# Both halves of a two-matmul accumulation wait for the later of their inputs

## The reference

```python
x = x + layernorm(attention(layernorm(x)))     # 16 heads of 8, 1024 keys
x = x + layernorm(ffn(layernorm(x)))

# ffn: three cycles, each of them on all 1024 tokens
gf = global_net(mean of x over the tokens)
for _ in range(3):
    h = gelu(out @ w1 + b1)      # 256 -> 256
    h = gelu(h @ w2 + b2)        # 256 -> 128, contracted over 256
    h = gelu(h @ w3 + b3)        # 128 -> 64
    tf = sigmoid(h @ w4 + b4)    # 64 -> 1
    coupling = 0.1 + adaptive_range * (0.7 * gf + 0.3 * tf - 0.5) * 2.0
    out = out + coupling * twist(out)
```

## Time and profile before

| | us |
|---|---|
| median of 3 runs | 3420.03 |
| the profiled execution, its own time | 3420.04 |
| its span (first to last instruction) | 3418.2 |
| TensorE busy | 3280.1 (96%) |
| VectorE busy | 2961.0 (87%) |
| ScalarE busy | 2896.0 (85%) |
| GpSimd busy | 976.6 (29%) |

### The profile page before, as it was taken

How to read it: one execution, slowest core, us unless ns; L and a number is a source line. 1 busy time by engine, 2 the same in 40 slices (tenths; PEclk the granted TensorE clock), 3 DMA queues, 4 the chain that set the end, 5 groups by cost and what they waited for, 6 DMA issues and landing times.

```text
span 3418.2 us, 55797 instructions
## 1 busy us (share of the span) xinstructions
PE 3280.1 (96%) x19328; PEld 931.1 (27%) x19328; DVE 2961.0 (87%) x5517; ACT 2896.0 (85%) x3806; POOL 976.6 (29%) x1382
## 2 busy tenths in 40 slices
PE   6989999999999999999999999999999999999987
PEld 2222232322323232232322323232232322323222
DVE  7999989888898988989888898988989888898942
ACT  3868979798897979889798897979989798896975
POOL 5012060421506033060421406033060421505024
PEclk7998999999999999999999999999999999999999
DMA  3111111121112111111121111111121121111001
GB/s 89 26 41 43 37 44 32 43 49 43 51 33 54 39 49 43 43 50 32 43 50 43 51 33 50 41 46 47 36 57 33 43 49 44 38 32 50 7 22 37
DMA packets 97337, 144.71 MB, mean 42 GB/s; under 512 B 49312, under 2 KB 59936, under 8 KB 89248
## 3 DMA queue, kind: packets, MB, share of 16 engines
q1 hardware_dynamic: 93360, 123.83, 13.7%
q0 software_dynamic: 3696, 17.31, 2.7%
HBM read 34.61 MB, written 32.51 MB: 20 GB/s over the span
## 4 chain that ended last, share of the span: by engine, by line
PE 69%; DVE 14%; ACT 8%; issue 4%; SPq 2%; POOL 2%; DMA 1%; DVEq 0%; POOLq 0%
PE heads_ps L503 24%; PE ring_ps L470 15%; PE scoresT_ps L488 11%; DVE max_parts L949 10%; PE scoresT_ps L590 7%; ACT p_sb L700 4%; PE scoresT_ps L595 3%; DVE stats L960 2%; PE scoresT_ps L598 2%; ACT headsT L709 1%; PE scoresT_ps L601 1%; PE ring_ps L532 1%; SPq L337 1%; PE scoresT_ps L518 1%; PE heads_ps L470 1%
## 5 line engine op out<-in xcount | busy, mean ns | idle before, releaser
L949 DVE TENSOR_REDUCE max_parts<-ring_ps 128x1 f32<-128x512 f32 x3741 | 2365.5, 682 | 230.0 <-PE ring_ps L470 171.1
L700 ACT ACTIVATE p_sb<-scoresT_ps 128x1024 f32<-128x1024 f32 x2048 | 1970.2, 1025 | 84.6 <-PE scoresT_ps L488 60.8
L470 PE MATMUL ring_ps<-k_rows,q_rows 48*128 48x512 bf16 x3741 | 1078.0, 385 | 23.5 <-DVE max_parts L949 14.4
L503 PE MATMUL heads_ps<-p_sb,v_sb 128*9 128x512 f32 x8192 | 1073.3, 596 | 17.9 <-ACT headsT L709 11.9
L488 PE MATMUL scoresT_ps<-q_rows,k_rows 51*128 51x512 bf16 x4096 | 1021.8, 384 | 15.0 <-ACT p_sb L700 7.5
L470 PEld LDWEIGHTS ring_ps<-k_rows,q_rows 48*128 48x128 bf16 x3741 | 263.5, 94 | 1319.9 <-DVE max_parts L949 1209.6
L1210 POOL CAST max_wide<-max_all 128x16 bf16<-128x16 f32 x128 | 25.1, 196 | 1753.7 <-DVE max_all L955 1753.7
L590 PE MATMUL scoresT_ps<-state,w 128*128 128x512 f32 x736 | 365.4, 619 | 5.9 <-DVE state L1013 3.9
L488 PEld LDWEIGHTS scoresT_ps<-q_rows,k_rows 51*128 51x128 bf16 x4096 | 207.7, 94 | 243.7 <-ACT p_sb L700 219.9
L811 ACT ACTIVATE p_sb<-scoresT_ps,b 128x512 f32<-128x512 f32 x180 | 123.5, 686 | 165.6 <-PE scoresT_ps L590 164.6
L503 PEld LDWEIGHTS heads_ps<-p_sb,v_sb 128*9 128x9 f32 x8192 | 124.7, 89 | 289.6 <-issue 278.6
(11 more groups left out here) (206 smaller groups left out, 2757.7 us busy)
## 6 DMA issues: line engine op xcount, KB each, us to landing
q_rows<-parts SPq DMA_DIRECT2D x744, 32.0 KB
k_rows<-parts SPq DMA_DIRECT2D x744, 32.0 KB
x_sb<-in_x SPq DMA_DIRECT2D x16, 1024.0 KB, 4.9
x_in<-in_x SPq DMA_DIRECT2D x15, 1024.0 KB, 5.1
out<-x_sb SPq DMA_DIRECT2D x15, 1024.0 KB, 3.9
out<-x_in POOLq DMA_DIRECT2D x15, 1024.0 KB, 7.8
q_rows<-max_rows SPq DMA_DIRECT2D x512, 3.0 KB
feat_h<-headsT SPq DMA_DIRECT2D x512, 16.0 KB
```

What stands on the lines that cost most here:

```text
L470: e.matmul(ring_bank(max_taken, u + 1), q_rows[rows, slot, pair, h * BANK + qb * P:h * BANK + (qb + 1) * P], k_rows[rows, slot, pair, kh * ...
L503: m = e.matmul(heads_ps[32 * j:32 * j + DH + 1, :], v_sb[:, b % 2, kb, 4 * (group % NG) + j, 0:DH + 1], p_sb[:, n % 2, j, :], start=(kb == ...
L700: e.activation(p_sb[:, n % 2, 2 * two:2 * two + 2, :].rearrange("p h n -> p (h n)"), scoresT_ps[:, 2 * two * BANK:(2 * two + 2) * BANK], A ...
L949: e.tensor_reduce(max_parts[:, gi % 2, kh, col:col + 1], bank_of(max_taken, u + 1), AX.X, ALU.max).then_inc(max_taken, 1)
```

## The change

In layer 2 the wait for the hidden features leaves the loop over f. One wait, for the later of the two gelus (m = 0 and m = 1), stands ahead of both matmuls. Operands, order of the matmuls, banks and the semaphore's increments stay as they are.

```diff
                 if layer == 2:
+                    e.wait_ge(hid_done[k], max(end_of(before, cycle, 1, c, m) for m in range(2)))
                     for f in range(2):
-                        e.wait_ge(hid_done[k], end_of(before, cycle, 1, c, f))
                         o = e.matmul(ps, w2[:, f, :], hidden[k][:, 0, 2 * c + f, :], start=(f == 0), stop=(f == 1))
```

## The result

The changed kernel takes 3441.31 us (median of 6 runs, 3439.81 to 3444.48) against 3420.03 (6 runs, 3418.41 to 3421.84): a ratio of 1.0063, 95% interval 1.0053 to 1.0074. The forecast was 3435.9 with a range of 3429 to 3441. The direction is right, and so is the mechanism in the stages; the size is too small, above all in the ending: the median lies 0.3 us above the range, and the loss is 21.3 us instead of 15.9.

What follows compares the result with a forecast made beforehand. TensorE was taken to bound the coupling stages (busy 67.64 of 69.10 us), with nothing behind winning delays back. 7.4 + 5.8 + 0.3 + 2.4 = 15.9 us on 3420.0 gave 3435.9 us, range 3429 to 3441.

Steps and rivals of the forecast that it cites:

- The pairs in the stages: Coupling stages, c = 0: 0.53 us per delayed pair; 7.4 us for cycle 2, 5.8 for cycle 0, 0.3 for cycle 1.
- The ending: Pairs of batches 14 and 15: 1.7 + 0.5 + 0.2 = 2.4 us, with bounds of 0 and 5.2.
- the clock: TensorE: its granted clock falling where it is 1.00 now was named as a sign that the prediction is wrong; no size.
- Half absorbed: Rival, cycle 0 of the stages: VectorE's reductions take up its delay; 5.8 us less, 3430.1 us; chance 0.10.
- not slower: Rival: the attention stage makes the stages' lateness good; 3420.0 to 3422.4 us; chance 0.05, of which 0.01 for faster.
- It costs more: Rival: nothing covered in stages 0, 8, 9, whole 0.86 in the ending, costlier restarts; up to 3443.1 us; chance 0.08.
- the pull-ahead: TensorE: first weight load done before the wait ends, 0.11 us less in 25 pairs, 3433.1 us; left out of the sum.

Runs made afterwards that it cites:

- e3: Kernel before with the joined wait only in cycle 0, c = 0, of the 14 coupling stages; 3428.59 us, one run.
- e8: Changed kernel with layer 2 no longer waiting separately for its bank; 3438.74 us, ratio 1.0055.
- e1: Kernel before with the joined wait only in the ending (batches 14 and 15); 3426.3 us, ratio 1.0012.
- e10: Changed kernel with two added matmuls ahead of each joined c = 0 wait of the ending; 3442.96 us, ratio 1.0062.
- e6: Changed kernel with BEAT_UNITS putting three max units ahead of the c = 0 pairs in cycles 0 and 2, none behind; 3428.07 us, ratio 1.002.
- e12: Changed kernel once more, unaltered, timed against the kernel before; 3443.37 us, ratio 1.0065.
- e9: Kernel before with three added matmuls ahead of each c = 0 layer 2 of the ending; 3427.86 us, ratio 1.002.
- e2: Kernel before with the joined wait only in the 14 coupling stages; 3437.07 us, ratio 1.0044.
- e4: Kernel before with the joined wait only in cycle 2, c = 0, of the 14 coupling stages; 3430.76 us, one run.
- e5: Kernel before with the wait joined only in the 61 of 96 pairs whose gelu was already early; 3420.67 us, ratio 0.9999.
- e7: Kernel before with BEAT_UNITS putting three max units ahead of the c = 0 pairs in cycles 0 and 2, none behind; 3417.78 us, ratio 0.9992.
- e11: The kernel of e7 again, in more rounds, against the kernel before; 3418.32 us, ratio 0.9989.

## Why the prediction was too low

**The pairs in the stages: right, 1.4 us short.** The offsets of gelu and load gave 0.53 us for cycle 0 and e3 measures 0.53. In cycle 2 I took 0.05 us from gelu to load as well; it is 0.11 there, where another wait stands ahead (e8), so 14 x 0.59 = 8.3 us instead of 7.4. Cycle 0 cost its whole 0.53 in the first stage too (e3), where I had taken it as covered because the chain of before ran past the pair: that the chain goes elsewhere did not mean that TensorE had time to spare. That batch 9's stage lost only 0.2 us is chance, since the late DMA that held it before did not hold it after. The sum of all stages is 14.9 us in the trace against 13.5 forecast.

**The ending: the failed step, 5.1 us instead of 2.4.** Two things are in it: the waits, 3.15 us instead of 2.4, and a fall of TensorE's clock, 1.7 us, for which my sum had nothing. The first is an error of mine in "TensorE would be ready for its next load at 3370.90 + 1.40 = 3372.30, and that load waits until 3372.30 today: nothing is lost". I compared weight loads that stand in different places. A load that does not wait is pulled under the pass before it, a load that waits is followed by 0.11 us and then its pass. By passes the next layer would start at 3370.90 + 0.06 + 0.11 + 4 x 0.43 = 3372.79, against 3372.30 + 0.11 = 3372.41: 0.4 us. In cycle 2 the same sum is 3390.34 against 3389.49, 0.85 instead of 0.5. The rows for TensorE's passes in cycle 2, before:

```profile
3387.51 2.07 PE L595 MATMUL scoresT_ps<-q_rows,w 128*128 128x512 f32 x4
3389.41 1.95 PE L590 MATMUL heads_ps<-state,w 128*128 128x512 f32 x4
```

and after:

```profile
3408.22 1.96 PE L595 MATMUL scoresT_ps<-q_rows,w 128*128 128x512 f32 x4 [0.87 <-ACT q_rows L811]
3410.01 1.45 PE L590 MATMUL heads_ps<-state,w 128*128 128x512 f32 x3
```

Before, L590 starts behind a wait of its own, with its load in front of it; after, its load at 3409.59 lies under the last pass of L595. Taken at the first loads of the c = 1 pairs, the lag behind before grows by 0.08, 0.15 and 0.85 us over batch 14's three cycles, by 0.92 in batch 15's cycle 0 and by 0.85 in its cycle 2; in its cycle 1 it is 2.0, of which 0.3 is the wait. That makes 3.15 us for the waits. Another 0.2 comes behind the last pair; it is absent in e1, e8 and e10, which have the same waits, so it is not theirs. Against the forecast, batch 15's pairs cost 0.92, 0.3 and 0.85 instead of 0.86, 0 and 0.5, and batch 14's 0.08, 0.15 and 0.85 instead of 0.2, 0 and 0.86.

The second is the other 1.7 us of that cycle 1, the clock. Windows after, and below it the same place of before, between the c = 1 layer 4 and the next cycle's layer 1:

```profile
3383.80:3387.20 3.40, 3.40 (x5) 1.31 (x5) 0.69 (x1) 1.50 (x2) 3.14 (x5) 0.50 0.00 0
```

```profile
3365.30:3369.30 4.00, 3.93 (x9) 1.74 (x10) 0.69 (x1) 2.30 (x4) 3.65 (x6) 1.00 0.00 0
```

The granted clock is 0.50 there, the level of 1.2 GHz, and 1.00 before, 2.4 GHz. In the timeline after, the passes of L590 then take twice their time:

```profile
3381.60 0.59 PE L598 MATMUL heads_ps<-q_rows,w 128*64 128x512 f32 x1
...
3383.05 1.36 PE L601 MATMUL ring_ps<-q_rows,w_all 64*128 64x512 f32 x2 [0.86 <-ACT q_rows L815]
3384.34 3.37 PE L590 MATMUL scoresT_ps<-state,w 128*128 128x512 f32 x4
```

The price is read between batch 15's first and second pair: 21.62 us in the changed kernel, e1, e6 and e12, and 19.94 in e8 and e10, where the clock does not fall there: 1.7 us. In e8 and e10 it falls at 103 us instead, for twice as long, and the step from the second pair to the third is 21.2 instead of 17.9: 3.3 us. My text gave the clock as something that would make the prediction wrong, with no price. Without these 1.7 us the median would have been 3439.6, inside the range.

Is that chance? A half-speed stretch between 60 and 115 us after the last exponential is in all 7 traces of kernels whose ending pairs are displaced (changed, e1, e6, e8, e9, e10, e12) and in none of the 7 others (before, e2, e3, e4, e5, e7, e11). So it belongs to the displacement, as far as 14 traces tell. It is not the idle time at the joined wait that does it (e9, e10). In all seven the fall begins 0.2 to 0.9 us after the second of two waits of 0.86 us, those for layers 3 and 4. But the same two waits stand in all 14 traces at the same distance from each other, and in the other seven TensorE passes them at full clock. What about the displacement makes the clock fall there stays open.

**The base and the scatter.** The six runs of before lay at 3420.03; 59 more, in three groups, have medians of 3420.97 to 3422.33. That explains nothing of the loss, since both kernels were timed together: e12 lost 22.1 us beside a before of 3421.29. Single stretches at half clock, at the start of an attention stage or in the last coupling stage, come and go between executions, with 1.5 to 1.7 us each (128.0 against 129.65 us for batch 11 of before; in e12 and e10 it is batch 3). They are in the traces of 13 of the 14 runs (not in e6), and the changed kernel's runs went from 3439.45 to 3446.28, so a range for it has to allow for them.

The parts of the miss of 5.4 us are then 1.4 in the stages, 0.75 for the waits of the ending, 1.7 for the clock there, 0.2 behind its last pair, and 1.3 of scatter (0.8 in places where nothing was changed, 0.5 between the profiled execution and the median).

**The rivals.** "Half absorbed" is refuted by e3, "not slower" by e2 to e4. "It costs more" (up to 3443.1) comes near the number, but partly for wrong reasons: stage 0 was paid, and four of the ending's six pairs cost more than forecast, but only three of the six cost about their whole 0.86; a restart cost nothing in cycle 0 (0.53 in e3) and 0.06 where a second wait stood ahead, and the stage of batch 8 was covered. That rival had no term for the clock. That a wait holds its weight load too, against which I weighed the pull-ahead in the Trainium skill ("TensorE: Matmul & The Clock Gate", section "Step-by-step: what each phase is for"), the trace after confirms in each of the 35 pairs that wait for their gelu: the first load comes 0.05 or 0.11 us behind it. In that section's terms only the loads without a wait were pulled ahead.

## What to carry to other kernels

Before two waits are merged, look at what the engine does between them: here the first matmul (0.86 us) was the cover for the second one's input, and where the later input came 0.48 us after the first load, merging cost just these 0.48 us and the release, with nothing behind to win them back. Where both inputs were early it cost nothing. When a delay is worked out on TensorE, count in passes: weight loads slide under the pass before them or not, and mislead by 0.3 us a time. And when work is moved in time, allow for the clock: here its fall cost 1.7 to 3.3 us, more than any single wait.

## What the runs showed of the hardware

TensorE's load started 0.05 us after the end of the activation that it waited for. Where another wait stood ahead of it, on the same semaphore or on another, it was 0.11, with a wait instruction of 51 ns in between (e8). The granted clock fell to half right behind two waits of 0.86 us that TensorE passes at full clock in other kernels, and two or three small matmuls put in the place of an earlier wait did not prevent it. In the kernel before, the stages of batches 8 and 9 were 1 us longer behind the DMA `feat_h`; with three max units ahead of the pairs and none behind (e7, e11) these two were not, but batch 11's was 0.7 longer behind another, `sums_h`, which took 3.07 us instead of 2.36. The coupling stretches of e7 and e11 are 2.9 and 1.7 us shorter in sum than those of before. That is the likely source of their 3 us, but one trace each, with DMAs that come late in some executions, does not show it.
